# The deviation of a channel norm, spread by the tensor engine or by transfers: a shifted-window transformer block on one core

## The reference

```python
xn = _ln2d(x, norm1_g, norm1_b)          # norm over the 64 channels of a position
xn = roll(xn, (-4, -4)); windows = window_partition(xn, 8)      # 8 x 8 positions
attn_out = _mha(windows, in_w, in_b, out_w, out_b) @ proj_w.T + proj_b
y = x + roll(window_reverse(attn_out), (4, 4))
mu = mean(y, channels); var = mean((y - mu) ** 2, channels)     # second norm
z = (y - mu) * rsqrt(var + 1e-6) * norm2_g + norm2_b
z = gelu(fc1_w z + fc1_b)                # 64 -> 256 channels, per position
out = y + fc2_w z + fc2_b                # 256 -> 64 channels
```

## Time and profile before

| | us |
|---|---|
| median of 3 runs (88.52 to 90.08) | 88.78 |
| the profiled execution, its own time | 87.22 |
| its span, first to last instruction | 85.2 |

### The profile page before, as it was taken

One profiled execution on the slowest core, in us unless ns is written; L12 is line 12 of the kernel. 1 busy time (PEld: TensorE's weight loads), 2 busy tenths in 40 slices (PEclk: granted clock), 3 DMA queues, 4 the chain that ended last, 5 costly groups with the idle time before them and its releaser, 6 DMA issues.

```text
span 85.2 us, 4265 instructions
## 1 busy us (share of the span) xinstructions
PE 79.6 (93%) x1786; PEld 48.0 (56%) x1786; DVE 64.7 (76%) x208; ACT 53.0 (62%) x89; POOL 46.8 (55%) x58
## 2 busy tenths in 40 slices
PE   5999999889999999799999999999999999999950
PEld 5987757555865767467566637465464423533420
DVE  4999998969789989989789999997943944333260
ACT  0396798879888476588288356664587664725400
POOL 7988829989862972997634675787204041300000
PEclk9999999999999999999999999999999999999998
DMA  0799600121101122101021120000000000032042
GB/s 19 203 331 439 258 31 8 36 66 33 53 32 53 51 84 78 53 1 38 32 100 56 52 64 6 8 0 8 0 8 0 0 0 0 13 118 86 38 162 84
DMA packets 3490, 5.75 MB, mean 67 GB/s; under 512 B 944, under 2 KB 1712, under 8 KB 3344
## 3 DMA queue, kind: packets, MB, share of 16 engines
q1 hardware_dynamic: 2608, 3.08, 10.9%
q10 hardware_dynamic: 864, 2.40, 7.3%
HBM read 2.66 MB, written 1.05 MB: 44 GB/s over the span
## 4 chain that ended last, share of the span: by engine, by line
PE 65%; DVE 18%; issue 8%; DMA 3%; ACT 2%; SPq 1%; DVEq 0%; ACTq 0%
PE ps_s L333 14%; PE ps_u L426 6%; PE ps_u L499 5%; DVE row_max L656 4%; PE ps_m L307 4%; PE ps_s L483 4%; PE ps_t L333 3%; PE ps_t L483 3%; DMA masked<-qk 3%; PE ps_o L467 3%; PE ps_m L483 2%; PE ps_t L409 2%; PE ps_m L297 2%; PE ps_o L499 2%; PE ps_o L442 2%
## 5 line engine op out<-in xcount | busy, mean ns | idle before, releaser
L1058 POOL TENSOR_TENSOR max_x<-max_t,early 128x512 bf16<-128x512 bf16 x14 | 14.7, 1048 | 10.6 <-DVE max_t L669 10.6
L656 DVE TENSOR_REDUCE row_max<-ps_s 128x16 f32<-128x1024 f32 x15 | 18.1, 1209 | 2.5 <-PE ps_s L333 2.2
L915 ACT ACTIVATE probs<-ps_t 128x1024 f32<-128x1024 f32 x13 | 13.3, 1023 | 8.8 <-PE ps_t L409 8.4
L333 PE MATMUL ps_s<-masked,qk 32*64 32x256 f32 x240 | 16.9, 387 | 1.0 <-ACT probs L915 0.4
L333 PE MATMUL ps_t<-masked,qk 32*64 32x256 f32 x224 | 15.5, 387 | 0.0
L1067 POOL TENSOR_TENSOR rstd<-y_var,minus_half 128x4 f32<-128x4 f32 x8 | 8.1, 1010 | 9.9 <-DVE y_var L719 9.8
L333 PEld LDWEIGHTS ps_s<-masked,qk 32*64 32x64 f32 x240 | 8.1, 131 | 5.9 <-issue 2.9
L426 PE MATMUL ps_u<-probs,vz 128*32 128x64 f32 x512 | 10.5, 222 | 0.0
L426 PEld LDWEIGHTS ps_u<-probs,vz 128*32 128x32 f32 x512 | 7.9, 109 | 3.1 <-issue 2.7
L1043 POOL TENSOR_TENSOR rstd<-var,minus_half 128x4 f32<-128x4 f32 x8 | 8.3, 1043 | 1.0 <-DVE var L644 0.4
L282 PE MATMUL ps_t<-zeros 128*128 128x128 f32 x32 | 6.9, 376 | 1.0 <-DVE zeros L817 1.0
(11 more groups left out here) (111 smaller groups left out, 150.6 us busy)
## 6 DMA issues: line engine op xcount, KB each, us to landing
masked<-qk SPq DMA_DIRECT2D x38, 32.0 KB, 2.0
x_ch<-x_ch_d ACTq DMA_DIRECT2D x1, 1024.0 KB, 8.0
out_d<-result SPq DMA_DIRECT2D x3, 256.0 KB, 2.5
x_tok<-x_tok_d ACTq DMA_DIRECT2D x1, 512.0 KB, 6.0
masked<-qk SPq DMA_DIRECT2D x8, 64.0 KB, 2.4
late<-late_d ACTq DMA_DIRECT2D x1, 352.0 KB, 5.2
x_tok<-x_tok_d SPq DMA_DIRECT2D x2, 128.0 KB, 3.4
x_tok<-x_tok_d ACTq DMA_DIRECT2D x1, 256.0 KB, 4.8
```

What stands on the lines that cost most here:

```text
L333: return nc.tensor.matmul(ps[o:o + L, g, n * TOK:(n + 1) * TOK], qk[r:r + RG, b, w, t], masked[r:r + RG, b, :, w, t], start=(n == 0), stop ...
L656: nc.vector.tensor_reduce(row_max[:, w, 0:16], score_bank(k, w)[:].rearrange("q g (h j) -> q (g h) j", j=L), axis=AX.X, op=ALU.max).then_i ...
L915: nc.scalar.activation(probs[:, w, :], scores_t_bank(k, w)[:].rearrange("q g c -> q (g c)"), ACT.Exp).then_inc(probs_done, 1)
L1058: nc.gpsimd.tensor_tensor(max_x[:, k % 2, w, :].rearrange("q (n i) -> q n i", n=16), bf16_high(max_t[:, w, :]).unsqueeze(1).to_broadcast([ ...
```

## The change

Tiles 2, 3 and 4 (`FAR`) get their spread in another way. `rstd2` of such a tile is written to a small array in memory (`rows_d`, 2 x 128 x 2 numbers), read back with each window column's 256 numbers repeated over 64 partitions into `rstd2_x`, and POOL multiplies `y` by it (`ln2_scale_far`). SP issues the three transfers of each of these tiles behind all its masking transfers. PE's `y_spread` and DVE's `ln2_scale` of the three tiles are gone. `rstd2` is stored with `w` outside `b`. `residual(0)` moves forward on DVE in slot 2, ahead of `transpose_sums(1)`. Waits on the scaled tiles are renumbered, and `project_out(4)` to `project_out(6)` no longer wait on one.

```diff
+        FAR = (2, 3, 4)
@@ sync
+            for k in FAR:
+                i = k - FAR[0]
+                sp.wait_ge(y_rstd_done, k + 1)
+                sp.dma_start(rows_d[i].rearrange("w q b -> q w b"), rstd2[:, k % 2]).then_inc(y_rows_written, 16)
+                sp.wait_ge(y_rows_written, 16 * (i + 1))
+                if i >= 2:
+                    sp.wait_ge(z_far_done, i - 1)
+                for w in range(2):
+                    sp.dma_start(rstd2_x[C * w:C * w + C, k % 2],
+                                 rows_d[i, w:w + 1].rearrange("w q b -> w (q b)").to_broadcast([C, TOK])).then_inc(y_rows_spread, 16)
@@ tensor
-                if 2 <= k < TILES - 1:
+                if k in (2, 3):
                     pe.wait_ge(z_done, k - 1)
...
             def fc1(s, m):
                 i = 2 * s + m
-                pe.wait_ge(z_done, 2 * s + 2)
+                pe.wait_ge(z_done, (2, 2, 3, 5)[s])
+                if s in (1, 2):
+                    pe.wait_ge(z_far_done, s + 1)
...
-                if t >= AHEAD:
+                if t >= AHEAD and t - AHEAD not in FAR:
                     y_spread(t - AHEAD)
@@ vector
-                if t > AHEAD:
+                if t > AHEAD and t - AHEAD - 1 not in FAR:
                     ln2_scale(t - AHEAD - 1)
...
+                if t == 2:
+                    residual(0)
                 if tile_ok(t - 1):
                     transpose_sums(t - 1)
...
-                if tile_ok(t - 2) and t - 2 not in SPLIT:
+                if t > 2 and t - 2 not in SPLIT:
                     residual(t - 2)
...
-            ln2_scale(TILES - 4)
@@ gpsimd
             def ln2_rstd(k):
                 pool.wait_ge(y_var_done, k + 1)
-                if k >= 2:
+                if k in (2, 3):
                     pool.wait_ge(y_rstd_spread, k - 1)
+                if k - 2 in FAR:
+                    pool.wait_ge(y_rows_written, 16 * (k - 3))
...
+            def ln2_scale_far(k):
+                i = k - FAR[0]
+                pool.wait_ge(y_rows_spread, 32 * (i + 1))
+                pool.wait_ge(y_done, k + 1)
+                nc.gpsimd.tensor_tensor(z_all[:, tokens(k)].rearrange("q (j b i) -> q j b i", j=4, b=BLK),
+                                        y_all[:, tokens(k)].rearrange("q (j b i) -> q j b i", j=4, b=BLK),
+                                        rstd2_x[:, k % 2].rearrange("q (j i b) -> q j b i", j=4, b=BLK),
+                                        op=ALU.mult).then_inc(z_far_done, 1)
...
                 if tile_ok(t + 1):
                     spread_max(t + 1, 0)
+                if t - AHEAD - 1 in FAR:
+                    ln2_scale_far(t - AHEAD - 1)
...
-            for k in range(TILES - 3, TILES):
-                ln2_rstd(k)
+            ln2_rstd(TILES - 3)
+            ln2_scale_far(TILES - 4)
+            ln2_rstd(TILES - 2)
+            ln2_rstd(TILES - 1)
```

More of the change, by code:

```diff
@@ L46, with swin_block_kernel @@
 LATE = HIDDEN + M2 * C + 2 * P + C
-def swin_block_kernel(nc, x_tok_d, x_ch_d, early_d, ident_d, late_d, out_d):
+def swin_block_kernel(nc, x_tok_d, x_ch_d, early_d, ident_d, late_d, rows_d, out_d):
     ctx = ExitStack()
@@ L121, in swin_block_kernel @@
         y_var = sb("y_var", [P, BLK, 32])
-        rstd2 = sb("rstd2", [P, 2, BLK, 2])
+        rstd2 = sb("rstd2", [P, 2, 2, BLK])
+        rstd2_x = sb("rstd2_x", [P, 2, TOK])
         z_all = sb("z_all", [P, ALL])
@@ L198, in swin_block_kernel @@
         z_done = sem("z_done")
+        y_rows_written = sem("y_rows_written")
+        y_rows_spread = sem("y_rows_spread")
+        z_far_done = sem("z_far_done")
         fc1_done = sem("fc1_done")
@@ L467, in y_spread @@
                         ins = nc.tensor.matmul(out[:, :, b, :],
-                                               rstd2[:, k % 2, b, c // C:c // C + 1].to_broadcast([P, cols]), ident,
+                                               rstd2[:, k % 2, c // C, b:b + 1].to_broadcast([P, cols]), ident,
                                                start=True, stop=True, tile_position=(0, c))
@@ L490, in fc2 @@
                 if s == 0:
-                    pe.wait_ge(z_done, TILES - 2)
+                    pe.wait_ge(z_done, 3)
                 if s == 1:
@@ L721, in ln2_scale @@
             def ln2_scale(k):
-                dve.wait_ge(y_rstd_spread, k + 2 if k == TILES - 2 else k + 1)
+                dve.wait_ge(y_rstd_spread, {0: 1, 1: 2, 5: 3, 6: 5, 7: 5}[k])
                 if k < TILES - 3:
@@ L1064, in ln2_rstd @@
                 pool.wait_ge(y_var_done, k + 1)
-                if k >= 2:
+                if k in (2, 3):
                     pool.wait_ge(y_rstd_spread, k - 1)
-                nc.gpsimd.tensor_tensor(rstd2[:, k % 2], y_var[:, :, 0:2],
-                                        minus_half[:].rearrange("q (n w) -> q n w", n=BLK), op=ALU.pow).then_inc(y_rstd_done, 1)
+                if k - 2 in FAR:
+                    pool.wait_ge(y_rows_written, 16 * (k - 3))
+                if k == TILES - 1:
+                    pool.wait_ge(y_rstd_spread, 3)
+                nc.gpsimd.tensor_tensor(rstd2[:, k % 2].rearrange("q w b -> q b w"), y_var[:, :, 0:2],
+                                        minus_half[:].rearrange("q (n w) -> q n w", n=BLK), op=ALU.pow).then_inc(y_rstd_done, 1)
+            def ln2_scale_far(k):
[6 more added lines that the diff above has]
+                                        op=ALU.mult).then_inc(z_far_done, 1)
             def residual(k):
@@ L1178 @@
         args.append(nc.dram_tensor(name, v.shape, mybir.dt.from_np(v.dtype), kind="ExternalInput").ap())
+    args.append(nc.dram_tensor("rows_d", (3, 2, P, BLK), F32, kind="Internal").ap())
     args.append(nc.dram_tensor("out_d", (P, ALL), F32, kind="ExternalOutput").ap())
```

## The result

The changed kernel takes 91.42 us in the median of 20 runs (88.25 to 94.68), the kernel before 88.65 in 20 runs beside it (86.75 to 90.60): slower, ratio 1.019 with a 95% interval of 1.012 to 1.026, outside the range that was forecast. The ratio compares the fastest executions of each kernel (here 3 of the 20 of the changed one, all within 1.5% of its fastest), the medians hold all; so they do not divide into each other. The profiled execution took 89.55 us, span 87.7, against 87.22 and 85.2, at a mean granted clock of 1.00.

A forecast was written before the change was run, and what follows sets the result against it. The prediction took DVE, nearly level with PE, as the bound up to 55.00 us and PE alone after it. Gains of 0.31 + 0.44 + 0.44 = 1.19 us, taken as 1.2 from the 88.78 median, gave 87.6 us, range 86.9 to 89.8.

The forecast's parts named there:

- SP and the transfers: SP's queue: per tile one write, a wait and two reads, with landings of 2.3 us taken from the masking transfers.
- T: Latency from POOL's `rstd2` to the landed `rstd2_x`: 5.3 us taken, bounds 4.0 to 8.7.
- 2.1 us to spare: Tile 4 scaled by 65.9, PE wanting it at 68.04 for the third step of `fc1`: 2.1 us left, so hidden.
- late rows: Rival at `fc1(2,0)`: rows come late, costing from T = 7.07, gain gone at 7.67; 89.9 us in the middle; chance 0.16.
- Tile 2 on DVE: Tile 2's scaling leaves DVE ahead of the score maximum that PE waits for: 0.31 us gained on the path.
- PE's two spreads: Spreads of tiles 3 and 4 leave PE's part of the chain after 55 us: 2 x 0.44 = 0.88 us gained.
- the sum: The forecast gain on DVE before 55 us and PE after it: 0.31 + 0.44 + 0.44 = 1.19 us.
- The residual: Tile 0's residual moved forward on DVE in slot 2: at most 0.2 us gained or 0.4 lost, taken as 0.
- rival C: Rival set for the experiments: the rest of the edit, such as the moved residual, eats the gain; no chance given.
- POOL against DVE: Rival: POOL's products of tiles 2 and 4 hold up DVE's attention products by 0.70 and 0.56; 88.2 us; chance 0.11.
- More than counted: Rival: tile 2's spread and scaling both on the path, plus 0.2 from the residual: 1.8 us, 87.0; chance 0.18.

The follow-up runs named there:

- the sixth experiment: The changed kernel with tile 4's row written to memory twice, one write behind the other, before its reads: 94.73 and 97.16 us.
- whole pieces: The changed kernel with 16-byte writes per partition and 2 KB row reads, right output: 87.86 us, ratio 0.996 to the kernel before; two later variants 0.987 and 0.991.

## Why the prediction was wrong

**The step that failed is "SP and the transfers": T.** It took 2.3 us per landing from the masking transfers and T = 5.3. Measured are 3.3 for the write and 3.2 for the read, and for tile 4 T = 7.1 and 8.0 in two executions, and 8.35 with POOL in another order; tile 2's row took 8.1 from when SP came free. All lie inside the bounds of 4.0 to 8.7; the value chosen was that of a near row in kind (a transfer on SP's queue), not of a transfer with as many or as small pieces. The reason given, that median transfers are what idle queues should give, is refuted: tile 4's reads (67.21 to 71.02) and the second write of the sixth experiment (3.4 us) had no other transfer of SP's in flight beside them, and they were long. The "2.1 us to spare" of the next step went with it.

**The rival "late rows" is what happened**, by its place and its chain: POOL stands before tile 2's product (1.05 us), the last spread of maxima and tile 4's power wait behind it, and PE stands before the third step of `fc1`. It had a chance of 0.16 and the gain gone from T = 7.67. That threshold is about right: at 7.1 the stand (0.58) eats half of the gain, at 8.0 (1.35) more than all. (With tile 2's 8.1 and tile 4's 7.1 its formula gives a stand of 1.1.) What the rival did not price is the clock, which the sixth experiment shows falling behind a long stand: of the changed kernel's 20 executions 11 have a mean granted clock below 0.985, with a median of 92.77 us, the other 9 a median of 89.86. The profiled one is of the 9, so the medians (2.8 us apart) tell more of a usual execution than the ratio does. The page named beside it ("DMA: Bandwidth & Descriptors", section "Specifications", of the Trainium skill) has the DMA engine read, modify and write below 512 bytes. It gives no time for that, and no run shows such a step. Pieces of 16 bytes landed in 1.4 to 3.4 us over four kernels, against 2.9 to 3.7 for twice as many of 8. Small pieces may be a part of it, and waiting behind other transfers another: several writes were issued while the reads of the tile before were still landing, and landed just behind them (61.33 behind 61.21 in the changed kernel, 63.68 behind 63.58 with 16-byte pieces). The runs do not separate the two.

**The gain was there.** Tile 2 on DVE: 0.31 forecast, 0.33 to 0.34 measured, in every kernel that takes that tile by memory. PE's two spreads: 0.88 forecast, 0.70 to 0.74 measured, and 0.53 with POOL in another order and 8-byte pieces. The rest of PE's stage was not followed up. In the profiled execution the stages that the sum counts still gain 0.64 us with the stand in; what makes that execution longer lies in slots that the sum put at 0.

**The residual** was put at 0, between 0.2 gained and 0.4 lost. In its slot it costs 0.06. Whether it also makes PE's stops of the next slots likelier, which is rival C, is open: of ten profiled executions with it the two intervals after are long in eight, of three without it in one. No experiment had enough runs to say, and none was the changed kernel with the residual alone put back.

**POOL against DVE** did not happen in the changed kernel, whose late products miss DVE's. Where the rows were on time it did, even at the size that was feared (0.48 us on DVE, against half of 0.70). It cost nothing on PE's path (5.74 us against 5.72). So the rule cited for it ("SBUF — State Buffer", section "SBUF: two separate sides", of the Trainium skill: who starts first keeps the ports) agrees with rows of this case: the one that started first lost nothing, both times. The other lost 0.22 and 0.48 us, less than the 0.36 and 0.61 for which the first one still ran; and in the earlier trace rows the loser was the one listed first, by 0.02 us.

**"More than counted"** did not come: the two stages gave 1.06 us, not 1.8.

**What stays open.** The stops of PE under "issue" are most of what separates the two profiled executions, and they keep the kernel without transfers above its stages' sum. That the stand comes from the late row is shown: it grows with one more write and is gone where nobody waits and where tile 4 goes by PE, and gone or small (0.19) with whole pieces. That it makes the time a loss is shown by the kernels without it (0.987, 1.002, 0.996 against 1.019), with one exception: the kernel without transfers (1.012 with 1.002 to 1.021) can't be told from the changed one by its ratio, though its median is 0.1 us above the kernel before and the changed one's 2.8. What causes the stops is not shown, and no experiment was aimed at them.

## What to carry to other kernels

Before a value goes through memory to be spread, count its landings: the round trip has two in series, and for 2 KB written it took 7.0 to 8.4 us here, and 5.8 to 7.5 with whole pieces. Where the trace has no transfer of that form, put the chance on the upper bound, or leave the last, tightest consumer on the old path. And a consumer in the middle of an engine's queue makes one late row hold the next: put it behind the work that starts the next row. And test apart what an edit carries along: the moved residual was worth nothing in the sum, and its part in the loss is still open.

## What the runs showed of the hardware

- A stand of PE can cost twice. After 4.89 us of standing the granted clock was 0.54 for some 5 us, 2.1 us more; stands of 0.51 to 1.35 us left it at 1.00 in the profiled executions. Executions with a mean granted clock below 0.985 are 17 of 34 in the three kernels with a stand over 0.5 us (13 of 26 for the changed one), against 3 of 110 in all others of the experiments, the kernel before among them.
- 256 pieces of 8 bytes to memory land in 2.9 to 3.7 us (the changed kernel twice, and three variants of it), 128 of 16 bytes in 1.4 to 2.7 in two kernels and in 2.7 to 3.4 in two others. One row of 1 KB read by 64 partitions lands in 2.6 to 4.6, 64 different rows in 2.5 to 3.1 (one execution).
- The issue of one read took SP 2.46 us in one execution and 2.54 in another, against 0.54 in the median.
- POOL's two-input product takes 0.73 to 0.74 us with its second operand in strides of 8 bytes, and 0.85 to 0.88 in strides of 16; beside a product of DVE that started just ahead it takes 0.93 to 0.97.
